# Mixture-of-experts loop: a tile's first-layer matrix and biases read from DRAM at a register's address instead of copied by VectorE from a resident table

## The reference, cut to what matters

```python
# layer 0
one_hot = jax.nn.one_hot(jnp.argmax(logits, axis=-1), E, dtype=xf.dtype)
h = jax.nn.gelu(jnp.einsum('td,edh->teh', xf, w1), approximate=True)
y = jnp.einsum('teh,ehd->ted', h, w2)
out = jnp.einsum('te,ted->td', one_hot, y)
...
# layer 1
top_v, top_i = jax.lax.top_k(probs, K)
combine = jnp.sum(jax.nn.one_hot(top_i, E, dtype=xt.dtype) * top_v[..., None], axis=1)
for e in range(E):
    h = jax.nn.gelu(xt @ W1[e] + b1[e], approximate=False) @ W2[e] + b2[e]
    out = out + combine[:, e:e + 1] * h
```

## Time and profile before

| what | value |
|---|---|
| device time, median of 3 runs | 4948.01 us (4946.1 to 4949.84) |
| span of the profiled execution, first to last instruction | 4944.1 us |
| PE busy | 3835.4 us (78%) |
| DVE busy | 3465.1 us (70%) |
| POOL busy / ACT busy | 2386.9 us (48%) / 2341.8 us (47%) |
| mean granted TensorE clock | 0.900 |
| SP's DMA queue, packet time as a share of the 16 engines' span | 18.8% |

### The profile page before, as it was taken

The page is one execution under the profiler, slowest core; times in us unless marked ns, Lnnn a source line. Parts: engine busy times, 40 slices in busy tenths (PEclk is TensorE's granted clock), DMA queues, the critical chain, the costliest instruction groups (busy, mean ns, idle before and its releaser), DMA issues. The chain is left out here.

```text
span 4944.1 us, 90876 instructions
## 1 busy us (share of the span) xinstructions
PE 3835.4 (78%) x25840; PEld 2735.3 (55%) x25840; DVE 3465.1 (70%) x9524; ACT 2341.8 (47%) x5537; POOL 2386.9 (48%) x3900
## 2 busy tenths in 40 slices
PE   7889797779999799568869937567775887799365
PEld 5666565656666466456646626422332665466265
DVE  7887775666666676566658856669998664588566
ACT  3444464355666466234436624345553454366243
POOL 5666442534344442446643354367776662233453
PEclk9999898789999899679979959779998999899698
DMA  6000332100000232133323311212121330133113
GB/s 234 0 0 1 112 124 76 52 20 1 0 0 1 72 124 94 39 124 107 107 80 117 110 38 47 73 48 65 63 62 64 114 117 28 51 120 112 36 46 87
DMA packets 244547, 341.24 MB, mean 69 GB/s; under 512 B 26976, under 2 KB 187120, under 8 KB 243120
## 3 DMA queue, kind: packets, MB, share of 16 engines
q1 hardware_dynamic: 230960, 309.19, 18.8%
q0 software_dynamic: 13184, 27.22, 1.6%
HBM read 182.77 MB, written 147.26 MB: 67 GB/s over the span
## 5 line engine op out<-in xcount | busy, mean ns | idle before, releaser
L522 DVE TENSOR_REDUCE l0att_rowmax<-l0att_S 128x2 f32<-128x512 f32 x512 | 339.8, 687 | 125.2 <-PE l0att_S L701 122.9
L893 POOL TENSOR_TENSOR wb_prob<-wb_prob,wb_rden 128x128 f32<-128x128 f32 (+1 forms) x512 | 248.2, 506 | 360.7 <-DVE wb_rden L1070 360.3
L522 DVE TENSOR_REDUCE l1ffn_rowmax<-l1ffn_S 128x2 f32<-128x512 f32 x512 | 337.6, 686 | 87.2 <-PE l1ffn_S L701 83.1
L1983 POOL TENSOR_TENSOR ssm_hc<-core_AW_all,ssm_Cs 128x512 f32<-128x512 f32 x256 | 320.8, 1268 | 131.2 <-DVE core_AW_all L2129 98.1
L1434 POOL DMA_INDIRECT results<-e_y,e_back x220 | 213.7, 971 | 289.4 <-DVE e_y L1662 269.9
L935 ACT ACTIVATE wb_prob<-wb_biased,wb_nmax 128x128 f32<-128x128 f32 (+1 forms) x512 | 228.6, 447 | 236.0 <-DVE wb_nmax L1063 233.6
L2228 PE MATMUL ssm_Y<-ssm_hc,core_ident 128*128 128x512 f32 x512 | 287.8, 672 | 56.8 <-POOL ssm_hc L1983 31.1
L2129 DVE TENSOR_TENSOR_SCAN core_AW_all<-core_AW_all,ssm_U 128x512 f32<-128x512 f32 x256 | 310.6, 1213 | 1.0 <-ACT core_AW_all L2072 0.6
L701 PE MATMUL l1ffn_S<-l1ffn_K,l1ffn_Q 128*128 128x512 f32 x512 | 251.0, 494 | 75.1 <-DVE l1ffn_rowmax L522 42.3
L1775 PE MATMUL e_H<-e_xT,e_W1s 128*128 128x128 f32 x1760 | 252.0, 288 | 70.2 <-issue 50.6
L701 PE MATMUL l0att_S<-l0att_K,l0att_Q 128*128 128x512 f32 x512 | 248.6, 489 | 60.4 <-DMA l0att_K<-bounce 47.5
(11 more groups left out here) (498 smaller groups left out, 11511.3 us busy)
## 6 DMA issues: line engine op xcount, KB each, us to landing
bounce<-l0att_parts SPq DMA_DIRECT2D x128, 256.0 KB, 2.8
bounce<-l1ffn_parts SPq DMA_DIRECT2D x128, 256.0 KB, 2.8
ssm_Cs<-c_rows SPq DMA_DIRECT2D x128, 256.0 KB, 3.1
routed<-core_Y SPq DMA_DIRECT2D x8, 2048.0 KB, 24.8
l0att_Q<-bounce SPq DMA_DIRECT2D x128, 128.0 KB
l0att_K<-bounce SPq DMA_DIRECT2D x128, 128.0 KB
bounce<-l1att_parts SPq DMA_DIRECT2D x64, 256.0 KB, 2.8
l1ffn_Q<-bounce SPq DMA_DIRECT2D x128, 128.0 KB
```

The costliest lines, as they stand in the source:

```text
L522: dve.tensor_reduce(out=rowmax[:, jp, qt, 2 * pair:2 * pair + 2], in_=S[a % 2][:].rearrange("p (j k) -> p j k", j=2)[:, :, 0:keys(qt)], op ...
L893: ins = pool.tensor_tensor(out=prob[:, w_ % NP, a:b], in0=prob[:, w_ % NP, a:b], in1=rden[:, w_ % NP, n:n + 1].to_broadcast([P, b - a]), o ...
L1983: pool.tensor_tensor(out=hc[:, u % 4], in0=hs[:, u % 4], in1=Cs[:, n % 4], op=ALU.mult)\
```

## The change

A tile's first-layer matrix is no longer kept on chip. The slots `W1s` become a ring of six, like `got`, and SP fills them from DRAM with a DMA at a register's address. In layer 1 a row of the table in DRAM holds 512 values of the matrix, 4 of the first bias and 128 of the second bias (644 values, 322 KB a tile); in layer 0 it holds the 512 values (256 KB a tile). ACT reads its bias column, and DVE the second bias, out of the same slot. `weights(j)` is gone from DVE, and so are its register load, `b1s`, `b2_all`, `core.W1` and `core.b1` with their loads.

```diff
-        W1s = sb("W1s", [P, 2, FC * P])
-        b1s = sb("b1s", [P, 3, FC]) if b1 is not None else None
-        b2_all = sb("b2_all", [P, E, D]) if b2 is not None else None
+        B1, B2 = FC * P, FC * P + FC
+        W1s = sb("W1s", [P, RING, B2 + D if biases else B1])
...
             sp.wait_ge(offsets_made.sem, 1)
-            for b in range(2):
-                sp.wait_ge(rows_sent[b].sem, SENDS * GROUPS // 2)
             for j in range(NT):
-                await_(sp, x_made, j - RING + 1)
+                if j % 2 == 0:
+                    _, where = nc.values_load_multi_w_load_instructions(
+                        where_i[0:1, j:j + 2, :].rearrange("p t w -> p (t w)"), engines=[mybir.EngineType.SP],
+                        min_val=0, max_val=E * REGION - P, skip_runtime_bounds_check_because=CLAMPED)
+                first, w1_row = where[2 * (j % 2):2 * (j % 2) + 2]
                 await_(sp, y_taken, j - RING + 1)
-                await_(sp, back_ready, j - RING + 1)
-                first = sp.value_load(offset_i[0:1, j:j + 1], min_val=0, max_val=E * REGION - P)
+                sp.dma_start(W1s[:, j % RING, :], first_layer[bass.ds(w1_row, P), :]).then_inc(w1_in[j % RING].sem, 16)
+                if j == 0:
+                    for b in range(2):
+                        sp.wait_ge(rows_sent[b].sem, SENDS * GROUPS // 2)
                 sp.dma_start(got[:, j % RING, :], core.routed[bass.ds(first, P), :]).then_inc(fetched[j % RING].sem, 16)
...
-                dve.tensor_copy(offset_i[:], tab[:, 2]).then_inc(offsets_made.sem, 1)
+                step(dve.tensor_copy(where_i[:, 0:NT, 0], tab[:, 2]))
+                run(dve.tensor_scalar(where_i[:, 0:NT, 1], tab[:, 0], float(P), None, ALU.mult))
+                dve.sem_inc(offsets_made.sem, 1)
...
-            def weights(j):
-                e = expert[j] = dve.value_load(expert_i[0:1, j:j + 1], min_val=0, max_val=E - 1)
-                await_(dve, hid_made, j - 1)
-                if b1 is not None:
-                    await_(dve, acted, j - 2)
-                    step(dve.tensor_copy(b1s[:, j % 3], ...))
-                    settle()
-                dve.tensor_copy(W1s[:, j % 2], core.W1[:, bass.ds(e, 1), :].rearrange("p o f -> p (o f)"))\
-                    .then_inc(w1_copied.sem, 1)
...
-            for j in range(NT + 2):
-                if j < NT:
-                    weights(j)
-                if j >= 2:
-                    give(j - 2)
+            for j in range(NT):
+                give(j)
...
             def hidden_layer(j):
                 pe.wait_ge(x_taken.sem, j + 1)
-                pe.wait_ge(w1_copied.sem, j + 1)
+                pe.wait_ge(w1_in[j % RING].sem, 16 * (j // RING + 1))
                 await_(pe, acted, j - 1)
...
-    sp.dma_start(core.W1[:], a[which + "_W1"].rearrange("e d f -> d e f")).then_inc(core.moe_loaded.sem, 16)
```

More of the change, by code:

```diff
@@ L1275, in experts @@
     RING, ENDS = 6, 4
+    CLAMPED = "tables() takes the minimum of each entry and the last row that a tile can start at"
     with ExitStack() as ctx:
@@ L1316, in experts @@
         xT = sb("xT", [P, 2, P])
[L1317 to L1321 removed]
+        B1, B2 = FC * P, FC * P + FC
+        W1s = sb("W1s", [P, RING, B2 + D if biases else B1])
+        biased = sb("biased", [P, 2, D]) if biases else None
         hidden = sb("hidden", [P, 2, FC, P])
@@ L1340, in experts @@
         fetched = [sig(f"fetched{b}") for b in range(RING)]
+        w1_in = [sig(f"w1_in{b}") for b in range(RING)]
         x_made, x_taken = sig("x_made"), sig("x_taken")
-        w1_copied, hid_made, acted, y_made, y_taken, back_ready = (
-            sig("w1_copied"), sig("hid_made"), sig("acted"), sig("y_made"), sig("y_taken"),
-            sig("back_ready"))
+        hid_made, acted, y_made, y_taken, back_ready = (
+            sig("hid_made"), sig("acted"), sig("y_made"), sig("y_taken"), sig("back_ready"))
         given = sig("given")
@@ L1484, in activate @@
                 await_(act, y_made, j - 1)
-                if b1 is None:
+                if not biases:
                     ins = act.activation(hidden[:, j % 2].rearrange("p f t -> p (f t)"), H[j % 2][:], act_fn)
                 else:
-                    act.wait_ge(w1_copied.sem, j + 1)
+                    act.wait_ge(w1_in[j % RING].sem, 16 * (j // RING + 1))
                     for f in range(FC):
                         ins = act.activation(hidden[:, j % 2, f], H[j % 2][:, f * P:(f + 1) * P], act_fn,
-                                             bias=b1s[:, j % 3, f:f + 1])
+                                             bias=W1s[:, j % RING, B1 + f:B1 + f + 1])
                 ins.then_inc(acted.sem, 1)
@@ L1656, in give @@
                 dve.wait_ge(y_made.sem, j + 1)
-                if b2 is not None:
-                    dve.tensor_tensor(out=biased[:, j % 2], in0=YB[j % 2][:, 0:D],
-                                      in1=b2_all[:, bass.ds(expert[j], 1), :].rearrange("p o d -> p (o d)"),
+                if biases:
+                    dve.tensor_tensor(out=biased[:, j % 2], in0=YB[j % 2][:, 0:D], in1=W1s[:, j % RING, B2:B2 + D],
                                       op=ALU.add).then_inc(given.sem, 1)
                     dve.wait_ge(given.sem, j + 1)
-                dve.tensor_scalar(y[:, j % RING], YB[j % 2][:, 0:D] if b2 is None else biased[:, j % 2],
+                dve.tensor_scalar(y[:, j % RING], biased[:, j % 2] if biases else YB[j % 2][:, 0:D],
                                   got[:, j % RING, D + 1:D + 2], None, ALU.mult).then_inc(y_taken.sem, 1)
             step(dve.memset(before[:], 0.0))
+            if NT % 2:
+                step(dve.memset(where_i[:, NT:], 0.0))
             dve.memset(before16[:], 0.0).then_inc(based.sem, 1)
@@ L1679, in _ @@
             tables()
-            dve.wait_ge(w_loaded[0], w_loaded[1])
-            if b2 is not None:
-                dve.wait_ge(b2_in.sem, 16)
-            for j in range(NT + 2):
-                if j < NT:
-                    weights(j)
-                if j >= 2:
-                    give(j - 2)
+            for j in range(NT):
+                give(j)
             def join(g):
@@ L2577, in l0_experts @@
             experts(nc, core, f"e0{n}_", affine=(col("L0_ffn_ln2_w"), col("L0_ffn_ln2_b")), normed_in=True,
-                    w_loaded=(core.moe_loaded.sem, 32), gate=core.gates[:, 0, :], gate_b=core.gate_b[:, 0, :],
+                    w_loaded=(core.moe_loaded.sem, 16), first_layer=a["l0_W1"], gate=core.gates[:, 0, :], gate_b=core.gate_b[:, 0, :],
                     act_fn=ACT.Gelu_apprx_tanh, top=1, prefetch=prefetch)
         def l1_experts(n, out=None):
-            experts(nc, core, f"e1{n}_", affine=None, normed_in=False, w_loaded=(core.moe_loaded.sem, 64),
+            experts(nc, core, f"e1{n}_", affine=None, normed_in=False, w_loaded=(core.moe_loaded.sem, 32), first_layer=a["l1_W1"],
                     gate=core.gates[:, 1, :], gate_b=core.gate_b[:, 1, :], act_fn=ACT.Gelu, top=2,
-                    b1=core.b1, b2=a["b2"], out=out, out_norm=(row("L1_ffn_ln2_g"), row("L1_ffn_ln2_b")))
+                    biases=True, out=out, out_norm=(row("L1_ffn_ln2_g"), row("L1_ffn_ln2_b")))
         def l1_attention(n, prefetch=None):
```

25 lines of the change are left out of this document (9 added, 16 removed).

## The result

The changed kernel takes 4881.3 us, median of 4 runs (4875.08 to 4891.6), against 4947.4 (4946.1 to 4949.84) before: a ratio of 0.9872, 95% interval 0.9859 to 0.9885. The profiled execution is the slowest of the four, 4891.6 us with a span of 4889.8, so 54.3 us of span are to be explained in what follows.

A forecast was written before the change was run, and what follows sets the result against it. Layer 1 was taken to be bound by a chain through DVE's copies, layer 0 nearly by PE. Loops save 108 us, less 4 for POOL's additions, plus 2 at starts: 106 off 4948.0 gives 4842 us, range 4830 to 4872 (0.8).

The forecast's parts named there:

- The chain and the floor: Layer-1 loops: PE waits in series for DVE's matrix copy, 2.30 us a tile; without copies PE's floor is 1.89.
- the rival in which the copy was not the cause: Layer-1 loops: PE's own sequencer makes the 0.36 us gap, which stays; 4898 us, its band with mild DMA limit 0.08.
- the forecast's 73.5 and 0.85: Layer-0 loop: 5.50 + 36 x 1.89 = 73.5 us; 0.85 us is taken off the last load's start.
- the sum had 134.05: Layer-1 loop: 4.65 + 68 x 1.89 = 133.2 us, before the 0.85 us taken off the last load's start.
- A second chain: Rival, layer 1: 0.19 us idle stays on each of 140 steps, 27 us lost, 4869; 0.20 together with POOL block.
- GpSimd's additions: Layer-1 loops: POOL's additions can still delay DVE's `back`; charged 2 us a loop, 4 in all.
- The DMA added: All four loops: per-tile matrix DMAs are covered by the ring's lead and cost 0.
- 6T = D + 3T + 0.86: Ring of six: tile period T against D, from y(j-6) done to turn j; at 1.89 it allows D = 4.8 us.
- D is 3.2 us at most by these rows: Loops: time from freed slot to the tile's turn, 2.7 us plus queueing behind the matrix; 1.6 below what is allowed.
- the ring is too short: Rival: `got` waits behind matrices, loops run at DMA latency; at D = 7.0, 4992 us, slower; chance 0.04.
- a mild DMA limit: Case sharing the band 4885 to 4938 with the rival that the copy was not the cause; chance 0.08.
- The rest of the program: Outside the four loops: dropped loads and one more `tables` operation cost 0; wrong about the place if time moves there.

The follow-up runs named there:

- the ring of 8: Changed kernel with a ring of 8 tiles in place of 6 in both experts functions; 4859.0 us, ratio 0.9833 to the kernel before.
- the halved read: Changed kernel reading only 161 KB of each tile's 322 KB layer-1 row, for timing alone; 4874.0 us, ratio 0.9858 to the kernel before.
- 192 or 64 memsets: Changed kernel plus 192 or 64 one-element memsets in VectorE's idle time at the start; 4866.9 us (0.9829) and 4866.2 us (0.9831).

## Why the prediction was wrong

**The chain and the floor: right.** The rows named the copy, from a gap of 0.07 us, as what held PE. With a copy put back out of the chain, 28.5 us of it cost nothing, and the rival in which the copy was not the cause is out. The floor of 1.89 us is there in single turns (the transposes at 3099.51 and 3101.41 are 1.90 apart). With the ring of 8 the layer-0 loops take 74.3 us, as the forecast's 73.5 and 0.85 have it. The layer-1 loops take 137.5 and 138.0 where the sum had 134.05: 3.7 us each stay. In the first of them 0.8 us lie in the first two steps (5.43 us from the first to the third hidden layer, where the forecast took 4.65), and the rest is some 0.04 us a step, half of which the next point explains; what is left was not traced. A second chain that costs 0.19 us on every step is not there: from 3060 to 3105 us PE does 402 matmuls in 45 us, 1.90 us for the 17 of a tile.

**GpSimd's additions: charged 2 us a loop, about right as far as is known.** With the ring of 8, the stretch 3000 to 3050 us (with additions) holds 438 matmuls, 1.94 us a tile. Against the 1.90 us of the stretch without additions that is 0.04 us a tile, 1.4 us over the 35 or so tiles that have them. The 128 x 1 operation still took 1.17 us at 4760.57 beside an addition, as the Trainium skill's rule (SBUF — State Buffer, "Who interferes with whom") had it. `e_y`, whose operands are both in SBUF, was hit as well (1.34 us at 4750.04, 0.29 otherwise), which the prediction did not list.

**The DMA added, costed at 0: the step that failed.** The form of the equation stood, 6T = D + 3T + 0.86; the size of D did not. "D is 3.2 us at most by these rows" put 1.96 us from the issue of the rows to their use, and 0.5 for the matrix ahead. In the lap above it was 4.1 us from issue to arrival, and 5.4 us from the output of tile 47 to where the turn of tile 53 would have begun (the hidden layer's 3097.73 less the 0.1 us by which it follows its turn at full pace). Over the 56 turns from the fifteenth on, D has a mean of 5.1 us in this loop and 5.3 in the other. Two terms made the difference:

- The 1.96 us came from a row at the start of a loop and holds in the old layer-1 loop as well, where the rows land 2.0 us after their issue in the mean (61 tiles, DMA share 0.20). In the new loop, at a share of 0.81, it is 3.6. The 0.5 us assumed one matrix ahead, moved at the full rate of a stretch. But a tile is issued every 2.07 us and its parts take 3.6 and 3.9 us to land, so about two tiles are under way at once. By the halved read the bytes are what counts: 161 KB fewer gave back 10 us of each loop and 1.3 of the 1.6 us.
- PE does a register load of 0.7 us, with its register work, behind the wait for the rows and ahead of the hidden layer. It was named among PE's instructions, and not put into D. So the rows must be there 0.6 us before their turn, and the ring allowed 4.2 us and not 4.8. This term is read from the trace; no run takes it out by itself.

The 0.86 was too small too. It came from one pair of rows. From its turn to the end of its output a tile takes 7.3 us in the mean where 3T + 0.86 is 7.1; the constant is 1.1 and not 0.86, and it is 1.1 to 1.2 in the kernels with the ring of 8 and with the halved read as well. D = 5.1 and 1.1 together make the measured 2.07 us, and of the 0.18 us above the floor about half comes from each of the two. What the 0.25 us in the constant are was not traced.

The rival "the ring is too short" had the mechanism in words, "`got` waits behind its own matrix and behind earlier ones", but in numbers it had only the end at which it turns the result to slower, with 0.04. The milder form, D between 4.8 and 6.4, stood in the chances as "a mild DMA limit", together with another rival, with 0.08 and at 4885 to 4938, above what was measured. The measured 4881 falls into the band of 4856 to 4885, which had 0.20 for other reasons, a second chain or GpSimd's additions; that it does is luck. The sentence on the Trainium skill (DMA: Bandwidth & Descriptors, "Latency and other measured facts") put D at 5.0 and 13 us off the gain; measured are 5.1 to 5.3 and 23 us in layer 1. The page pointed the right way. I set it aside because no row of before showed such a latency; but no row of before showed a small DMA behind a large one at such a share either. What the page calls a latency was here mostly bytes, by the halved read.

**The rest of the program, costed at nothing: the second step that failed.** I had written that I would be wrong about the place if time moved outside the four loops, and it did, by 22.8 us. Of the copies' removal I counted the time and not the instructions. The first experts block lost 192 of VectorE's instructions, and all that follows moved up by as many. Of the 22.8 us, 17.4 are the five long passes, which 192 or 64 memsets took away wholly; the 5 us behind them may be scatter, since the same stretch takes 495.7 to 503.1 us over all runs. The Trainium skill (Runtime: NRT & Kernel Launch, "Instruction fetch mechanics") says that an engine's instructions are fetched in blocks while it runs, that VectorE's memory for them holds 512, and that a taken branch to a place that is no longer held makes it wait. The trace agrees on the branch: the pause of 2.59 us stands behind the branch back, in all five passes, and comes and goes with the packets. It disagrees with the blocks of 256 instructions that the page gives: a start at 51 past a multiple of 256 pauses and one at 243 doesn't, and a period of 128 fits all seven starts. Why the loop of 365 instructions is not held at some of these starts, the runs don't show.

So the 108 us of the loops became 54.3: less 27.4 in layer 1 and 3.2 in layer 0, less 22.8 and 1.1 outside, plus 0.8 at the start.

## What to carry to other kernels

When a resident table is replaced by a DMA, take the cover from the whole lap (issue, landing under the traffic that the loop itself makes, and what the consumer's sequencer still does behind the wait). Here the landing grew from 2.0 to 3.6 us by the loop's own traffic, and two more slots in the ring were worth some 20 us. Issue first what is needed first, even when it is the small one. And when instructions are added or removed ahead of a hardware loop, look at that loop in both traces: its place in the instruction stream alone was worth 15 to 20 us here, and a change that is measured in such a program can carry that along.

## What the runs showed of the hardware

- A hardware loop of 365 VectorE instructions leaves VectorE idle for 2.5 to 2.8 us at each branch back, where it is 0.22 us otherwise, or not at all, by where it begins: no pauses at instructions 2419 and 2291, pauses at 2227, 2225 (the ring of 8 alone), 2355, 2353 and 2499. A pass with a pause brings five packets of 8.2 KB on the instruction queue (25 more over five such passes, in the kernel before with 80 memsets).
- In the changed kernel such a pause made the pass 2.6 to 4.1 us longer, with TensorE's granted clock at 0.94 in the 10 us around one of them. Without pauses each of the five passes took 78.36 us, to 0.01, in each of the kernels that have none.
- A tile of 65 KB behind 322 KB in the same queue landed 3.6 us after its issue (mean of 63) at a DMA share of 0.81, where it took 2.0 us (mean of 61) at a share of 0.20, and 2.3 us behind 161 KB. The share could rise to 0.87 (244 GB/s) with 0.8 us of waits on PE's weight loads in 100 us.
- 128 memsets of one element were busy for 3.03 us in all at the start of VectorE's program, 24 ns each, in a wait that had been 7.0 us.
